# Layer 1 attention of a four-layer kernel: band added on TensorE, softmax read from PSUM, division moved to GpSimd, values computed with channels on partitions

## The reference, cut to what matters

```python
q, k, v = heads(shift_token(x) @ wqkv)          # 8 heads of 64 channels
q = l2norm(q) * qs;  k = l2norm(k) * ksc
q, k = rotary_xpos(q, k)
# windows of 64: queries i look at keys j of their own and of the window before
sim = einsum('bhwid,bhwjd->bhwij', bq * 8.0, bk)
sim = where((i < j) | (i > j + 64) | (j == -1), -max, sim)
out = softmax(sim) @ bv
x = x + out @ wo
```

## Time and profile before

| | us |
|---|---|
| median of 3 runs | 5822.17 |
| lowest and highest run | 5820.59, 5825.25 |
| span of the profiled execution | 5822.4 |

### The profile page before, as it was taken

The page is one execution under the profiler, slowest core; times in us unless marked ns, Lnnn a source line. Parts: engine busy times, 40 slices in busy tenths (PEclk is TensorE's granted clock), DMA queues, the critical chain, the costliest instruction groups (busy, mean ns, idle before and its releaser), DMA issues. The chain is left out here.

```text
span 5822.4 us, 60164 instructions
## 1 busy us (share of the span) xinstructions
PE 4385.6 (75%) x16724; PEld 2482.1 (43%) x16724; DVE 4514.1 (78%) x8572; ACT 2924.5 (50%) x5085; POOL 2325.4 (40%) x1980
## 2 busy tenths in 40 slices
PE   5876778767787677876778767787678866788776
PEld 1533435344353443534435344353444524444344
DVE  3678966789657996579965799658995489955898
ACT  3544645446444564445644456444564445645455
POOL 0134631447204562045620456104661046610565
PEclk9998889978899888998889988998889998899888
DMA  2000000000000000000000000000000000000000
GB/s 99 1 1 2 1 3 1 1 2 1 3 1 0 2 1 3 1 1 2 1 3 1 2 1 1 3 1 2 1 1 3 1 2 1 1 3 1 2 1 2
DMA packets 3537, 22.97 MB, mean 4 GB/s; under 512 B 336, under 2 KB 336, under 8 KB 2640
## 3 DMA queue, kind: packets, MB, share of 16 engines
q1 hardware_dynamic: 3152, 18.59, 0.8%
HBM read 16.23 MB, written 2.36 MB: 3 GB/s over the span
## 5 line engine op out<-in xcount | busy, mean ns | idle before, releaser
L1622 POOL TENSOR_SCALAR l_pp<-l_sc,l_m 128x512 f32<-128x512 f32 x496 | 783.4, 1579 | 644.3 <-DVE l_m L1572 596.7
L1572 DVE MAX8 l_m<-l_wk 128x8 f32<-128x512 f32 x1536 | 980.6, 680 | 0.0
L224 PE MATMUL bank<-l_v,l_pt 128*128 128x99 f32 (+1 forms) x5888 | 871.4, 300 | 139.5 <-ACT l_pt L1362 114.7
L224 PEld LDWEIGHTS bank<-l_v,l_pt 128*128 128x128 f32 x5888 | 814.9, 216 | 196.7 <-ACT l_pt L1362 154.0
L1316 PE MATMUL bank<-consts,l_pp 128*128 128x128 f32 x2048 | 390.9, 323 | 526.3 <-POOL l_pp L1629 519.8
L1180 POOL TENSOR_TENSOR l_hc<-l_h,l_cn 128x1024 f32<-128x1024 f32 x128 | 302.3, 2362 | 989.0 <-DVE l_h L1130 989.0
L1316 PEld LDWEIGHTS bank<-consts,l_pp 128*128 128x128 f32 x2048 | 280.2, 165 | 959.7 <-POOL l_pp L1629 828.2
L224 PE MATMUL bank<-l_km,hold 128*128 128x512 f32 x1024 | 652.7, 727 | 43.3 <-DVE l_ol L1539 18.1
L1568 DVE MATCH_REPLACE8 l_wk<-l_m,l_wk 128x512 f32<-128x512 f32 x1024 | 684.1, 675 | 0.0
L1392 ACT ACTIVATE l_sc<-bank 128x512 f32<-128x512 f32 x512 | 303.3, 594 | 739.9 <-PE bank L224 738.5
L1629 POOL TENSOR_TENSOR l_pp<-l_pp,l_ex 128x512 f32<-128x512 f32 x496 | 631.0, 1272 | 26.4 <-ACT l_ex L1399 5.7
(11 more groups left out here) (350 smaller groups left out, 8065.6 us busy)
## 6 DMA issues: line engine op xcount, KB each, us to landing
weights<-weights_dram SPq DMA_DIRECT2D x1, 11014.0 KB, 29.0
hold<-x_dram SPq DMA_DIRECT2D x9, 256.0 KB, 2.6
out_dram<-x SPq DMA_DIRECT2D x9, 256.0 KB, 3.4
consts<-consts_dram SPq DMA_DIRECT2D x1, 1503.0 KB, 32.2
rotary<-consts_dram SPq DMA_DIRECT2D x1, 1024.0 KB, 34.1
```

The costliest lines, as they stand in the source:

```text
L224: return nc.tensor.matmul(o, lhsT, rhs, start=start, stop=stop)
L1572: nc.vector.max(m8[n % RM][:, k + 1], wk_[n % 2][:]).then_inc(S["top"], 1)
L1622: nc.gpsimd.tensor_scalar(pp[n % 2][:], sc[n % RS][:], m8[n % RM][:, 3, 0:1], None, ALU.is_ge).then_inc(S["kept"], 1)
```

## The change

The band is no longer added by VectorE. A bf16 copy of the band and a bf16 unit matrix are made once, and `score` starts each score tile with a matmul of the two (so the band is in PSUM) and adds the score product to it. VectorE takes the maximum straight from PSUM, with q not normalised; its reciprocal norm times 8 (`qrs`, one number per query and head) is the `scale` of ScalarE's Exp, which also reads PSUM, takes maximum times scale as its bias, and accumulates the row sums (`zs`). The Exp is four instructions a unit, since scale and bias differ by head. VectorE takes the reciprocal of the sums, and GpSimd multiplies the probabilities by it ahead of the transposes. The value product has the values as weights (64 columns) and the turned probabilities streaming, so its output has channels on partitions: `ot`, `oinv`, the column of ones and `turn_outputs` are gone, and ScalarE copies bank 6 + q%2 to `of`. The norms of q are made as columns (eight small passes with 2 columns for each n) with one Ln and one Exp of 128x32 for all four, and GpSimd's sum writes q into `qk` directly. In `attend` the scores of u + 2 come first.

```diff
+        band = ctx.enter_context(nc.sbuf_tensor("band", [128, WIN + 128], BF16))
+        eye = ctx.enter_context(nc.sbuf_tensor("eye", [128, 128], BF16))
...
                             for f in range(2):
                                 for s in range(2):
                                     g = 2 * f + s
-                                    r = mm(bank[2 * e + f][:, 256 * s + n0:256 * s + KW],
-                                           qk[64 * e:64 * e + 64, g * T + 128 * q:g * T + 128 * q + 128],
-                                           qk[64 * e:64 * e + 64, (4 + g) * T + lo:(4 + g) * T + 128 * q + 128])
-                                r.then_inc(S["score"], 1)
+                                    o = bank[2 * e + f][:, 256 * s + n0:256 * s + KW]
+                                    mm(o, eye[:], band[:, n0:KW], True, False)
+                                    r = mm(o, qk[64 * e:64 * e + 64, g * T + 128 * q:g * T + 128 * q + 128],
+                                           qk[64 * e:64 * e + 64, (4 + g) * T + lo:(4 + g) * T + 128 * q + 128], False, True)
+                            r.then_inc(S["score"], 1)
...
-                                        v2 = vt[:, q - 1 + d, 2 * j + e:2 * j + e + 2, :].rearrange("p h d -> p (h d)")
-                                        r = mm(bank[6 + e][:, 65 * j:65 * j + PW], pt[f][:, 2 * s + d], v2[:, 0:PW],
-                                               d == parts[0], d == 1)
+                                        r = mm(bank[6 + q % 2][64 * e:64 * e + 64, 128 * g:128 * g + 128],
+                                               vt[:, q - 1 + d, 2 * g + e], pt[f][:, 2 * s + d], d == parts[0], d == 1)
...
+                                if n < 4:
+                                    for q in range(NT):
+                                        r = mm(bank[4][:, 8 * n + 2 * q:8 * n + 2 * q + 2], sqq[n % 2][:, 128 * q:128 * q + 128],
+                                               C("head64")[:, 0:128:64])
+                                    r.then_inc(S["ss"], 1)
+                                    return
...
                             def exponent(u):
-                                e, n0 = u % 2, WIN if u >= 2 else 2 * WIN
-                                a.wait_ge(S["centred"], NU * i + u + 1)
-                                act(pe_[e][:, :, n0:256], pe_[e][:, :, n0:256], ACT.Exp).then_inc(S["exp"], 1)
+                                q, e = u // 2, u % 2
+                                k, n0 = NU * i + u, 0 if q else WIN
+                                a.wait_ge(S["shift"], k + 1)
+                                if k >= 2:
+                                    a.wait_ge(S["turned"], 2 * (k - 1))
+                                    a.wait_ge(S["rec"], 2 * (k - 1))
+                                for f in range(2):
+                                    for s in range(2):
+                                        g = 2 * f + s
+                                        r = act(pe_[e][:, g, WIN + n0:256], bank[2 * e + f][:, 256 * s + n0:256 * s + KW],
+                                                ACT.Exp, scale=qrs[:, g, q, e:e + 1], bias=shift[e][:, g:g + 1],
+                                                accum_out=zs[e][:, g:g + 1])
+                                    r.then_inc(S["exp"], 1)
...
+                                nc.vector.tensor_reduce(
+                                    nmax[e][:], banks[:, 2 * e:2 * e + 2].rearrange("p b (s j) -> p (b s) j", s=2)[:, :, n0:KW],
+                                    AX.X, ALU.max, negate=True).then_inc(S["max"], 1)
+                                v.wait_ge(S["max"], k + 1)
+                                tt(shift[e][:], nmax[e][:], qrs[:, :, q, e], ALU.mult).then_inc(S["shift"], 1)
...
+                                    nc.gpsimd.tensor_tensor(p, p, rec[e][:, 2 * f:2 * f + 2, None].to_broadcast([128, 2, KW - n0]),
+                                                            ALU.mult).then_inc(S["shared"], 1)
```

More of the change, by code:

```diff
@@ L496, in score @@
                             if u >= 2:
[L497 removed]
+                                pe.wait_ge(S["exp"], 2 * (k - 1))
                             for f in range(2):
@@ L510, in attend @@
                             parts = (0, 1) if q else (1,)
-                            pe.wait_ge(S["exp"], k + 1)
-                            if k:
-                                pe.wait_ge(S["pt"], 2 * k)
-                            if e and q:
-                                pe.wait_ge(S["of"], NT * i + q)
+                            if u + 2 < NU:
+                                score(i, u + 2)
                             for f in range(2):
+                                if k:
+                                    pe.wait_ge(S["pt"], 2 * (k - 1) + f + 1)
+                                pe.wait_ge(S["shared"], 2 * k + f + 1)
                                 for s in range(2):
@@ L669, in root @@
                             def root(n):
-                                k = 8 * i + n
-                                a.wait_ge(S["ss"], k + 1)
+                                k = 4 * i + n - 4
+                                if n < 3:
+                                    return
+                                a.wait_ge(S["ss"], 8 * i + n + 1)
+                                if n == 3:
+                                    flat = qrs[:].rearrange("p g q e -> p (g q e)")
+                                    if i:
+                                        a.wait_ge(S["shift"], NU * i)
+                                    act(flat, bank[4][:, 0:32], ACT.Ln, scale=NORM_SCALE, bias=C("floor")).then_inc(S["q_ln"], 1)
+                                    a.wait_ge(S["q_ln"], i + 1)
+                                    act(flat, flat, ACT.Exp, scale=-0.5, bias=C("norm_back")).then_inc(S["q_rs"], 1)
+                                    return
                                 if k >= 2:
@@ L713, in _ @@
                                 k = NU * i + u
+                                if u + 1 < NU:
+                                    exponent(u + 1)
                                 for f in range(2):
@@ new lines, in share @@
+                            def share(u):
+                                e, k = u % 2, NU * i + u
+                                for f in range(2):
+                                    v.wait_ge(S["exp"], 2 * k + f + 1)
+                                    if k >= 2:
+                                        v.wait_ge(S["shared"], 2 * (k - 2) + f + 1)
+                                    nc.vector.reciprocal(rec[e][:, 2 * f:2 * f + 2], zs[e][:, 2 * f:2 * f + 2]).then_inc(S["rec"], 1)
+                            v.wait_ge(S["q_rs"], i + 1)
```

122 lines of the change are left out of this document (54 added, 68 removed).

## The result

| | before | changed |
|---|---|---|
| median of 4 runs each, us | 5821.38 | 6032.22 |
| lowest and highest run, us | 5817.28, 5825.25 | 6018.59, 6071.09 |
| span of the profiled execution, us | 5822.4 | 6016.8 |

The ratio is 1.0375, interval 1.0342 to 1.0408: slower by 3.75%. The direction was forecast, the size was not: +211 us by the medians and +194 by the two profiles, where the sum gave +130, and 6032 lies just above the range that ended at 6030. The profiled execution of the changed kernel was the fastest of its four (6018.59 us), so the rows show the cheapest of the four.

The account below looks back on a forecast made before the run. TensorE in program order was taken as the bound; per stage -2.8 + 6.7 + 5.2 - 2.7 + 1.7 = +8.1 us, x16 = +130 us, so 5950 us, range 5880 to 6030.

Parts of the forecast that it names:

- Part 1: Projections: without the q rows' Ln, Exp and multiply, TensorE's gaps close or shrink; -2.8 us a stage, between 1.8 and 3.6.
- Part 2 and 3: Middle units: TensorE pays for each change between band and score rows; a unit 6.3 us, four plus 5.2 us.
- Rival A: Middle and opening: band matmuls run in the shadow of the scores without a drain; faster, 5770 us, chance 0.10.
- Part 4 and 5: Opening: scores of units 0 and 1 no longer overlap, plus 6.7 us; closing: units without scores, minus 2.7 us.
- Part 6: TensorE's clock: two stretches at 1.2 GHz a stage where 0.7 stood, 1.3 us each; plus 1.7 us, between 0 and 5.
- Rival B: Middle units: the clock falls again and again as changes idle the array; +6 to +8 us a stage, 6060 us, chance 0.10.
- Rival C: Projections: no gain, the roots of k alone hold the end; +1 us a stage, 5968 us, chance inside the sum's 0.74.
- Rival D: ScalarE in middle units: four short exponents cost over 1.2 us each, so ScalarE passes 6.3 us a unit; chance 0.02.

Follow-up runs that it names:

- e1: The changed kernel with each pair of score tiles getting its band from one matmul ahead of the scores; 5851.16 us, ratio 1.0057.
- e2: The changed kernel with each band made by two bf16 matmuls on the same 64 rows as its score; 5912.50 us, ratio 1.0155.
- e10: The changed kernel with one unread fp32 product filling TensorE's gap ahead of the first band; 6034.89 us, ratio 1.0368.
- e4: The changed kernel with two unread fp32 products in TensorE's wait for the first exponent; 5990.50 us, ratio 1.0297.
- e7: The changed kernel with bands grouped, also in the opening, scores between transposes and values, and reciprocals ahead of the next maximum; 5833.37 us, ratio 1.0022.
- e8: e7 with one unread fp32 product in TensorE's wait for the first exponent; 5778.61 us, ratio 0.9928 against the kernel before the change.

## Why the prediction was right in direction and wrong in size

**What bounds the attention** was read rightly: TensorE in program order, before and after. In the middle TensorE never waited for `shared` or `exp`.

**Part 1** (-2.8): from the first projection to the first score 31.53 us before (134.80 to 166.33) and 29.46 now (133.64 to 163.10), so -2.1. The gap at `Wk` shrank to 0.25 instead of closing, and the last one to 1.19 instead of about 1. That is the first depth. In the second the same way went from 31.33 to 30.28, only -1.05, because the last gap grew from 1.61 to 2.00 us:

```profile
272.69 0.69 DVE L799 SCALAR_TENSOR_TENSOR l_qk<-l_rn,l_of 128x512 f32<-128x512 f32 x1 [1.23 <-POOL l_of L887]
273.54 0.22 PE L227 MATMUL bank<-band,eye 128*128 128x128 bf16 x1 [2.00 <-DVE l_qk L799]
```

There VectorE's last multiply waits 1.23 us for GpSimd's sum, which the prediction held to be no longer late. The mean over the 16 stages is -1.6, under the lower bound of 1.8 that the part gave. The q norms hold (eight passes with 2 columns, 0.95 us wide).

**Part 2 and 3** (+5.2 for four middle units): a pair is 0.70 us, forecast 0.75 (0.57 in the opening, forecast 0.62); a unit 6.06 to 6.14, forecast 6.3. Four are 24.4 against 20.13: +4.3. The assumption that each change of rows is paid was right (e1, e2), at a slightly lower price. Rival A, no drain, falls with the first pair.

**Part 4 and 5** (+6.7 and -2.7): the closing took 11.11 us (216.51 to 227.62), forecast 11.2, -2.8. The opening has no stage at the full clock to be read from; what is left of +6.5 when the other parts are taken off, part 1 with its mean of -1.6, is +6.6. It is a remainder, not a measurement.

**Together** the parts without the clock gave +6.4 a stage, and the line through the stages gives +6.5. That it is so near is partly luck: part 1 missed by 1.2 us one way and the middle units by 0.9 the other.

**Part 6 is the step that failed** (+1.7 taken; +6.0 measured, 96 us over 16 stages against 27). Each low stretch was priced rightly: 1.3 us for 3.3 us at 1.2 GHz is 0.39 us for each, and the measured slope is 0.41. What was wrong is their length. The part took two stretches of the length that before had behind a wait, 6.6 us a stage in all; there were 17.1, from 10.2 to 30.7. The count was not too low: 25 stretches in the 16 stages, 1.6 a stage. It reasoned that a gap is what brings the clock down and that it comes back after 3.3 us, as it did in dense fp32 work. The changed kernel's alternating pairs can bring it down without a gap (e10) and then run on at the low one for up to 30 us, which a dense fill behind the opening shortens (e4). The upper end of this term, 5, was taken from nothing that alternates, since the trace of before had no such stretch, and it was too low.

**Rival B** came nearest, with its +6 to +8 on the sum and 6060 us (measured +4.4 on the sum); its mechanism differs: not a fall in each unit, but one or two stretches a stage, from the opening's pairs on or from the wait for the first exponent on. Its chance of 0.10 rested on the middle stretches at 1.00, which are of the old, dense order and so said little of the new one. **Rival C** is true in size: part 1 gained 1.2 us less than its sum, where C had 1. **Rival D** falls: four exponents are 1.8 to 1.9 us.

**What stays open**: why the low stretch lasts 10 us in one stage and 30 in another of the same kernel, and why the low stretches of e2, whose pairs no longer change rows, last 13.7 us a stage once a wait has set them off. Runs between which only the density of the pairs differs were not made.

## What to carry to other kernels

Matmuls that alternate between 64 and 128 rows pay a change each time, and they can take the clock down as well: order the products so that one tile shape runs as long as it can (here worth 181 us with the same arithmetic). When a change makes TensorE's work sparser, read the clock term from a sparse stretch or set its upper bound at the whole of the stretch, not at the length of the stretches of the dense kernel. Judge the place of a step again after its surroundings have changed: the same move of the scores cost 97 us and later gained 25.

## What the hardware showed that was not expected

- The granted clock fell in work without a wait over 0.32 us ahead of it (e10, the eight stages of the first depth). In the first stage of the changed kernel it stayed at 1.2 GHz for 30.7 us, and in the 25.23 us from 173.01 on TensorE was busy 25.04. The busy share of the profile does not tell whether the clock holds.
- One needless product of 0.86 us ahead of the first transposes took the low time from 6.2 to 1.5 us a stage (e7, e8) and the kernel from no gain to a gain of 0.7%. In the gap ahead of the pairs the same product did nothing (e10).
- Six changes of rows and two band loads fewer in a unit gave 0.89 us (2.82 against 1.93), so a change between a bf16 band and an fp32 score is 0.15 us at most.
- GpSimd's multiply of 384 fp32 columns by a broadcast operand is 826 ns, less than the 1.0 us that was scaled from 512 columns.
